# Four heads to a score unit, local mixes by two pairs, and feed-forward parts as streams of their own

## What is computed

```
# ATTN0, ATTN1: 16 heads of 8 channels
scores = einsum('bhqd,bhkd->bhqk', q, k) * scale      # ATTN1: rotary q and k, causal
out = softmax(scores) @ v
# LOCAL0, LOCAL1: 8 heads of 64 channels
h = shift_token(x); q, k, v = split(h @ wqkv)
q = l2norm(q) * qs; k = l2norm(k) * ks; q, k = rotary_xpos(q, k)
x = x + local_attention(q, k, v) @ wo
h = layernorm(shift_token(x)) * lg + lb
a, g = split(h @ w1 + b1); x = x + (a * gelu(g)) @ w2 + b2
```

## Time and profile before

| | |
|---|---|
| median of three runs | 3128.42 us (3126.73 to 3133.96) |
| profiled execution, its own time | 3130.85 us |
| its span, first to last instruction | 3128.7 us |
| granted clock of TensorE, mean | 0.957 |
| busy: TensorE, VectorE, ScalarE, GpSimd | 2816.9, 2411.2, 2147.9, 1548.2 us |

### The profile page before, as it was taken

How to read it: one execution, slowest core, us unless ns; L and a number is a source line. 1 busy time by engine, 2 the same in 40 slices (tenths; PEclk the granted TensorE clock), 3 DMA queues, 4 the chain that set the end, 5 groups by cost and what they waited for, 6 DMA issues and landing times.

```text
span 3128.7 us, 65895 instructions
## 1 busy us (share of the span) xinstructions
PE 2816.9 (90%) x22656; PEld 1976.8 (63%) x22656; DVE 2411.2 (77%) x6016; ACT 2147.9 (69%) x5956; POOL 1548.2 (49%) x1741
## 2 busy tenths in 40 slices
PE   3678999999999999999999999999999999998875
PEld 1455666666666666666666666666666666666553
DVE  3367888888888888888888888878888888777653
ACT  2356777777777777677777767777776777776653
POOL 1034554555545455554555554545555555545542
PEclk7689999999999999999999999999999999999987
DMA  2000000000000000000000000000000000000000
GB/s 67 3 3 4 5 6 6 5 6 6 6 5 7 6 4 6 6 6 6 5 7 6 5 6 6 6 5 7 6 5 6 6 6 5 6 4 4 4 5 5
DMA packets 41974, 21.76 MB, mean 7 GB/s; under 512 B 21131, under 2 KB 41013, under 8 KB 41653
## 3 DMA queue, kind: packets, MB, share of 16 engines
q1 hardware_dynamic: 41652, 17.55, 2.0%
HBM read 9.17 MB, written 4.19 MB: 4 GB/s over the span
## 4 chain that ended last, share of the span: by engine, by line
PE 43%; DVE 27%; ACT 19%; POOL 5%; issue 4%; DMA 0%; DVEq 0%; POOLq 0%; SPq 0%
DVE negmax L836 10%; ACT rawP L730 6%; ACT P L730 5%; PE bank L1050 5%; PE bank L1143 5%; PE bank L1151 4%; PE bank L1030 4%; PE bank L1096 3%; DVE ss L879 3%; PE bank L1159 3%; POOL rn L633 3%; PE bank L1130 2%; ACT probs L697 2%; PE bank L1085 2%; PE bank L1011 2%
## 5 line engine op out<-in xcount | busy, mean ns | idle before, releaser
L836 DVE TENSOR_REDUCE negmax<-bank 128x2 f32<-128x512 f32 (+1 forms) x896 | 554.4, 679 | 25.7 <-PE bank L1011 25.6
L697 ACT ACTIVATE probs<-bank 128x512 f32<-128x512 f32 (+1 forms) x1024 | 480.9, 568 | 131.8 <-PE bank L1030 129.5
L633 POOL TENSOR_TENSOR rn<-ss,minus_half 128x16 f32<-128x16 f32 x128 | 372.6, 2911 | 172.0 <-DVE ss L894 171.4
L582 POOL TENSOR_TENSOR veps<-moments,eps_tile 128x2 f32<-128x2 f32 x192 | 38.2, 199 | 785.4 <-DVE moments L788 785.4
L1085 PE MATMUL bank<-wqkv_sb,hS 128*128 128x512 f32 x768 | 390.9, 625 | 30.9 <-ACT P L730 12.7
L914 DVE TENSOR_REDUCE negmax<-bank 128x2 f32<-128x384 f32 (+1 forms) x384 | 211.7, 593 | 135.1 <-PE bank L1118 133.4
L600 POOL TENSOR_SCALAR_AFFINE_SELECT probs<-probs 128x256 f32<-128x256 f32 x512 | 225.2, 463 | 166.8 <-ACT probs L697 166.4
L1050 PE MATMUL bank<-probs,V 128*16 128x256 f32 (+1 forms) x4096 | 259.5, 373 | 24.4 <-ACT probs L697 22.2
L1011 PE MATMUL bank<-kT,qT 32*128 32x256 f32 (+1 forms) x2048 | 216.8, 324 | 25.7 <-DVE negmax L836 16.1
L1085 PEld LDWEIGHTS bank<-wqkv_sb,hS 128*128 128x128 f32 x768 | 131.9, 193 | 163.3 <-issue 125.6
L730 ACT ACTIVATE rawP<-bank,negmax 128x128 f32<-128x128 f32 x512 | 179.7, 376 | 79.7 <-DVE negmax L914 79.7
(11 more groups left out here) (138 smaller groups left out, 7299.2 us busy)
## 6 DMA issues: line engine op xcount, KB each, us to landing
xin<-x SPq DMA_DIRECT2D x32, 128.0 KB, 2.1
out<-xout SPq DMA_DIRECT2D x32, 128.0 KB, 1.8
V<-YB SPq DMA_DIRECT2D x64, 63.5 KB
wqkv_sb<-wqkv SPq DMA_DIRECT2D x1, 1536.0 KB
V<-YB SPq DMA_DIRECT2D x64, 0.2 KB
w_sb<-w SPq DMA_DIRECT2D x1, 682.0 KB
w_sb<-w SPq DMA_DIRECT2D x2, 256.0 KB
wo_sb<-wo SPq DMA_DIRECT2D x2, 256.0 KB
```

What stands on the lines that cost most here:

```text
L633: nc.gpsimd.tensor_tensor(rn[:, l, t].rearrange("p m h -> p (m h)"), ss[:, l, t].rearrange("p m h -> p (m h)"), minus_half[:], ALU.pow).th ...
L697: nc.scalar.activation(dst, src, ACT.Exp, scale=SCALE0 if k == ATTN0 else SCALE1)\
L836: nc.vector.reduce_max(negmax[:, k, t, head:head + 4 * many - 3:4], tile(u, e)[:, :].rearrange("p (h k) -> p h k", h=many), AX.X, negate=T ...
```

## The change

STREAMS becomes 6: the feed-forward parts of the local layers are streams FEED0 and FEED1, with buffers of their own (feed_h, feed_hT, up2T), and the gates are written into up2T. `maxes` and `scores` take four heads and four banks in a unit, so ATTN0 has four `maxes` instead of eight, ATTN1 three instead of six, and both have four `scores` instead of eight. `scores2` is a unit of two banks and one of four instead of three of two. `mix2` takes two pairs of heads, 512 columns of a bank, in two units instead of four. The clamp of the sums of squares is a maximum over pairs, of which the second element is a constant 1e-24, written to another tile. One more sequence is kept in XB and YB. All orders and bank lists are new; FIRST, TURNS and LAST have 472, 159 and 482 units in place of 339, 180 and 561, and ROUNDS is 26. The strings are cut here except for the start of TensorE's TURNS, and so are loops that change only in their bounds.

```diff
-STREAMS = 4
+STREAMS = 6
...
-KEPT_X, KEPT_Y = 5, 3
+KEPT_X, KEPT_Y = 6, 4
...
-ATTN0, ATTN1, LOCAL0, LOCAL1 = range(STREAMS)
...
-ROUNDS = 27
+ATTN0, ATTN1, LOCAL0, LOCAL1, FEED0, FEED1 = range(STREAMS)
...
+ROUNDS = 26
...
 TURNS = {
     "tensor": (
-        "1110330102222111002022103333333332222221122222200022011102333333333000313113100013333332222000332203"
-        "20033311111331220000322200122222201111222222333313000330011101333100033301222223"
+        "3333022222211222221120001130231011101333333003323002222220444433111110044341142222222233130000333330"
+        "01110112000001555553330500550222222333330211122020251333333"
...
-    units += [Unit("maxes", u, bank=2) for u in range(6 if rotary else 8)]
+    units += [Unit("maxes", u, bank=4) for u in range(3 if rotary else 4)]
     units += [Unit("negmax", m_hi=1, m_ready=1)]
     units += [Unit("turn_q", u, source="with maxima", bank=1) for u in range(2)]
+
+    def scores(g):
+        return Unit("scores", g, bank=4, **(dict(masked=4) if rotary else {}))
+
+    def mix(g):
+        return Unit("mix", g, bank=1)
+
     for g in range(GROUPS):
-        units += [Unit("scores", 2 * g + n, bank=2, **(dict(masked=2) if rotary else {})) for n in range(2)]
-        units += [Unit("mix", g, bank=1)]
+        units += [scores(g), mix(g)]
...
-def local_units(last):
+def local_units():
...
-    units += [Unit("scores2", u, bank=2, max_done=2) for u in range(3)]
+    units += [Unit("scores2", 0, bank=2, max_done=2), Unit("scores2", 1, bank=4, max_done=4)]
...
-    units += [turn_p(0), turn_p(1), turn_p(2), turn_p(3), mix2(0), turn_p(4), turn_p(5), mix2(1),
-              turn_p(6), turn_p(7), mix2(2), mix2(3)]
+    units += [turn_p(u) for u in range(4)] + [mix2(0)] + [turn_p(u) for u in range(4, 8)] + [mix2(1)]
     units += [Unit("project2", bank=1)]
-    units += [Unit("shift_rows", rows_in=2 * 16, rows_left=1)]
-    units += norm_units("h")
+    return units
+
+
+def feed_units(last):
+    units = [Unit("shift_rows", rows_in=2 * 16, rows_left=1)] + norm_units("h")
...
-    if k == ATTN1 and part < 2:
-        return 0, 0, GROUPS, part
-    n = part + 2 if k == ATTN1 else part
-    return n // 4, 2 * (n // 2 % 2), 2, n % 2
+    if k == ATTN1 and part == 0:
+        return 0, 0, GROUPS
+    n = part + 1 if k == ATTN1 else part
+    return n // 2, 2 * (n % 2), 2
...
-        ss = sb("ss", [P, 2, TT, 2, HEADS])
+        ss = sb("ss", [P, 2, TT, 2, HEADS, 2])
+        ss_kept = sb("ss_kept", [P, 2, TT, 2, HEADS])
...
-        up2T = rawA[:, :, 0:3 * SEQ].rearrange("p l (c q) -> p l c q", c=3)
+        feed_h = sb("feed_h", [P, 2, TT, DIM])
+        feed_hT = sb("feed_hT", [P, 2, SEQ])
+        up2T = sb("up2T", [P, 2, len(HTILES), SEQ])
...
-                    for sem, count in newest(taken(earlier(u, "project2"))):
+                    for sem, count in newest(taken(fellow(u, LOCAL0 + l, "project2")), taken_by_last(u, "down2")):
...
-                    flat = ss[:, l, t].rearrange("p m h -> p (m h)")
                     dve.wait_ge(sig("sums", src), so_far("sums", src) + 1)
-                    nc.vector.tensor_scalar(flat, flat, 1e-24, None, ALU.max).then_inc(sig("ss_ready", u), 1)
+                    nc.vector.reduce_max(ss_kept[:, l, t].rearrange("p m h -> p (m h)"), ss[:, l, t].rearrange("p m h e -> p (m h) e"), AX.X)\
+                        .then_inc(sig("ss_ready", u), 1)
...
+                elif u.kind == "mix2":
+                    dve.wait_ge(has_filled(u), uses(u))
+                    nc.vector.tensor_copy(o2T[:, l, 2 * u.part:2 * u.part + 2, :].rearrange("p c q -> p (c q)"), tile(u)[:])\
+                        .then_inc(has_emptied(u), 1)
...
-                    t, first, many, pair = max_part(k, u.part)
-                    for e in range(2):
-                        head = 4 * first + 2 * pair + e
+                    t, first, many = max_part(k, u.part)
...
                     for i in range(many):
-                        for e in range(2):
-                            rows = slice(32 * (2 * pair + e), 32 * (2 * pair + e) + 32)
+                        for e in range(4):
+                            rows = slice(32 * e, 32 * e + 32)
                             last = mm(tile(u, e)[:, i * keys:(i + 1) * keys], qT[rows, k, first + i, t * P:(t + 1) * P],
...
-                    g, pair = u.part // 2, u.part % 2
+                    g = u.part
...
-                        for sem, count in newest(*of("scores", 2 * g, 2 * g + 1)):
+                        for sem, count in newest(*of("scores", g)):
                             pe.wait_ge(sem, count)
                     else:
-                        pe.wait_ge(sig("masked", u), so_far("masked", u))
+                        src = earlier(u, "scores", g)
+                        pe.wait_ge(sig("masked", src), so_far("masked", src) + 4)
...
-                    for sem, count in newest(*(of("qkv2", 2, 5) if n == 0 else []), *of("turn_p", 2 * n, 2 * n + 1), free(u)):
-                        pe.wait_ge(sem, count)
-
-
-                    for q0, w, t, c0 in ((0, P + WINDOW, 0, 0), (P, P, 1, P + WINDOW)):
-                        for e in range(2):
-                            hd = 2 * n + e
-                            last = mm(tile(u)[64 * e:64 * e + 64, q0:q0 + w], V2[:, l, t, hd * HD:(hd + 1) * HD],
-                                      probs2[l][n % 2][:, e, c0:c0 + w], start=t == 0, stop=t == 1, skip_group_check=True)
+                    for sem, count in newest(*(of("qkv2", 2, 5) if n == 0 else []), *of("turn_p", *range(4 * n, 4 * n + 4)), free(u)):
+                        pe.wait_ge(sem, count)
+
+
+                    for i in range(2):
+                        for q0, w, t, c0 in ((0, P + WINDOW, 0, 0), (P, P, 1, P + WINDOW)):
+                            for e in range(2):
+                                hd = 4 * n + 2 * i + e
+                                at = i * SEQ + q0
+                                last = mm(tile(u)[64 * e:64 * e + 64, at:at + w], V2[:, l, t, hd * HD:(hd + 1) * HD],
+                                          probs2[l][i][:, e, c0:c0 + w], start=i == 0 and t == 0, stop=t == 1, skip_group_check=True)
```

275 lines of the change are left out of this document (141 added, 134 removed).

## The result

The changed kernel takes 3142.75 us (median of 8 runs, 3130.75 to 3145.66) against 3127.57 for the kernel before on the same chips: a ratio of 1.0043, 95% interval 1.0028 to 1.0059. It is slower by a little more than the 0.2% that can be told from nothing; 2970 us was predicted. The profiled execution took 3142.88 us.

A forecast was written before the change was run, and what follows sets the result against it. TensorE was taken to bound two thirds of a round, VectorE the rest. Work 79.2 + idle 7.0 + clock 1.2 = 87.4 us a round; fill 385 + rounds 2272 + drain 315 = 2972, said as 2970 us, range 2885 to 3060.

The forecast's parts named there:

- What bounds the kernel: Clean round of 89.6 us: TensorE bounds two thirds, VectorE the 29-us stretch with the maxima; local streams' latency a third limit.
- Part 1: Four heads at once on TensorE: 5.7 us less work a round, 84.9 to 79.2, by overlapping strips and fewer shape changes.
- Part 2: Smaller edits off TensorE's path: mix copies, clamp; VectorE 75.0 to about 73.5 us a round; 35 us if VectorE bound throughout.
- Part 3: Feed-forward as own streams: opens LOCAL's closed loop of 89.6 us a round and shortens the drain, 48 us taken.
- Part 4: Four-bank units' waits for free banks: 0.9, 2.0 and 0.8 us idle on TensorE, together 3.7 a round; elsewhere 0 to 3.
- term of idle time: TensorE's idle time in a clean round: 7.0 us instead of 4.7.
- The clock's 1.2 us: Mean round over clean round, put down to stretches at 1.2 GHz instead of 2.4; taken to stay at 1.2 us.
- The fill: Time before the steady rounds: 2.97 rounds of 87.4 us plus 125, 385 us; longer than 400 would show the forecast wrong.
- B: Rival: larger bank waits and VectorE's maxima stretch bind, about 2 us a round arrive, 3017 to 3036 us; chance 0.16.
- D: Rival: slower through four-bank waits, ten more short-reuse units a round, 3202 us at 0.8 us each; chance 0.10.
- E: Rival: strips overlap no better than now, or gain and waits cancel; no change, 3128 us; chance 0.02.

The follow-up runs named there:

- b_half: The kernel before, with half of the products of its 16-head maxes and scores units left out on TensorE: 3120.11 us, ratio 0.9991.
- b_look: The kernel before, with VectorE's maxima reductions looking at half of the keys: 3022.21 us, ratio 0.9670.
- a_pairs: The changed kernel, its four-bank units issuing heads 0 and 1 first, then 2 and 3: 3143.61 us, ratio 1.0051 to the kernel before.
- a_qkv: The changed kernel, with the local layers' first product in bfloat16 instead of float32: 3163.00 us, ratio 1.0138 to the kernel before.
- a_each: The changed kernel, its four-bank units waiting for each bank just before that bank's first product: 3141.71 us, ratio 1.0056 to the kernel before.
- b_qkv: The kernel before, with the local layers' first product in bfloat16 instead of float32: 3183.43 us, ratio 1.0204.
- b_qkv4: b_qkv with each of those bfloat16 products issued four times over, as useless work: 3123.40 us, ratio 1.0004 to the kernel before.
- a_keep: The changed kernel, with useless products laid into TensorE's waits of 0.9 and 2.0 us: 3164.25 us, ratio 1.0135 to the kernel before.

## Why the prediction was wrong

**What bounds the kernel: this step failed.** It read one 29-us stretch as VectorE's and the other two thirds of the round as TensorE's, because TensorE was busy there 58.8 of 60.6 us. Busy isn't bound: VectorE was 97% busy over 45 us. In b_half 1.9 us less TensorE work shortened the full-clock round by 0.3, and in the changed kernel, whose orders differ too, 5.5 us less shortened it by nothing, while 6.8 us less VectorE work (b_look) shortened it by 2.2. The chain's 43% for TensorE misled in the same way: b_half took 63 us off lines of that chain for nothing.

**Part 1** was right in size: 84.9 to 79.4 us a round (79.2 predicted), eight products in 0.44 us (timeline after):

```profile
1595.92 0.51 PE L1033 MATMUL bank<-kT,qT 32*128 32x256 f32 x8
1596.36 0.66 PE L1119 MATMUL bank<-ident_r,rawA 128*128 128x128 f32 x4
```

Its reason was half right: the order of heads plays no part (a_pairs).

**Part 2** had the direction, and the saving is nearly twice as large: VectorE 75.0 to 72.2 (73.5 predicted). The clamp (52.1 to 22.3 us in the kernel) and the mix copies (99.4 to 87.1) save what was forecast; another 31 us went from a multiplication that the change leaves as it is (rawA by rn, L902 before, 1185 to 947 ns each). It was costed as "not on TensorE's path", and in the kernel before the clamp turned out worth 21 us of the whole; in the new orders it is worth nothing. The step's figure for a VectorE-bound kernel, 35 us, was nearer than its verdict.

**Part 3** held in the drain and failed in the round. The last LOCAL1 took 46.6 us to its projection (about 45 predicted). In the rounds the loop closed again: LOCAL1's shift, its projection and its next shift, after:

```profile
1752.09 0.38 ACT L686 ACTIVATE hS<-bank 64x256 f32<-64x256 f32 x1
...
1843.22 0.38 ACT L686 ACTIVATE hS<-bank 64x256 f32<-64x256 f32 x1
...
1843.61 0.41 DVE L896 TENSOR_TENSOR YB<-bank,YB 128x256 f32<-128x256 f32 x1
```

91.5 us from shift to projection, where it was 64.8 with 28.8 of feed-forward behind it. The stream filled the round without its feed-forward part. Whether that is cause or consequence no run tells; a lighter product at its head (a_qkv) didn't help, in a run in which all of the middle 24 rounds had a stretch at half clock.

**Part 4** had the right place and the right first two waits (0.9 and 2.0; 0.88 and 1.99 measured). The third, put at 0.8 us for ScalarE, was 0.37 ahead of L1052, and not for ScalarE. **Its term of idle time failed**: 10.4 us, not 7.0. It walked one chain of bank waits and let "0 to 3" stand for the rest. The rest was 7.4: nine waits of 0.4 to 1.1 us and three smaller, two thirds of it in VectorE's stretch and 5.2 us for VectorE. The prediction's own mark, "wrong if the round is not under 88", was met.

**The clock's 1.2 us**, carried over unchanged, is 91.45 - 89.8 = 1.65 after. **The fill** came out at 423 us, beyond the mark of 400: 2.97 x 91.45 + 125 = 397 by its own formula, so of the 38 us about 12 come of the longer round and about 27 of the fill itself.

**Rivals.** B named the mechanism, VectorE's stretch, and still let 2 us arrive; 0 did. The rule of the Trainium skill (TensorEngine Tiling (Array Packing), section PSUM Bottleneck) that stood beside B, that copying out of PSUM may become the limit, agrees with the runs: only the kernels with a shorter reduction out of PSUM show the change's gain. D had the sign, by waits for four banks; by a_each the wait for all four at once is worth only 0.2 to 0.5 us a round of it. E, "the gain and the waits cancel", had 0.02 and came nearest: 5.5 us gained, 5.7 lost.

What stays open is why a full-clock round is 90 us at all: 6.8 us off VectorE shorten it by 2.2, 5.5 off TensorE by nothing, so neither of these two alone holds it, and which hand-overs do wasn't measured. No run took work off GpSimd, which had 5% of the chain before and is 82 us busier in the changed kernel (1548.2 to 1630.2), where no change was forecast. Nor did a run change the feed-forward streams alone.

## What to carry to other kernels

Before costing work taken off the busiest engine, take a like amount off each engine in turn, one short run each: here 219 us off VectorE brought 103 (some of it by the clock), 179 off ScalarE 22, and 63 off TensorE nothing, at busy shares of 77, 69 and 90%. Compare the rounds at equal granted clock too, since a gain can be hidden by the clock, as in a_each. In a kernel whose engines run in orders written out beforehand, bigger units mean fewer and longer hand-overs; when the consumer needs 2.5 us for what the producer makes in 0.5, a faster producer waits. Where TensorE's clock is at stake, look at the granted clock round by round and at the waits ahead of each fall, since a lighter TensorE can be the slower one.

## What the runs showed of the hardware that I hadn't expected

- 250 us less TensorE work in one product cost 2% (b_qkv), and the same time came back with useless products (b_qkv4). In the changed kernel the clock fell behind waits of 0.88 and 1.99 us, with no long idle time. The Trainium skill (TensorE: Matmul & The Clock Gate, section A second HAM failure mode: psum-queue depth-cycling) tells of a kernel whose short idle times between groups of products made the clock go up and down; this trace agrees, and with these two waits mostly filled (a_keep) the time at half clock went from 327 to 202 us.
- A tensor_scalar of 128 columns took 350 or 1129 ns, by what GpSimd did beside it. The Trainium skill (SBUF — State Buffer, section Who interferes with whom) says that a tensor_scalar in a two-port mode and a GpSimd instruction exclude each other for a whole instruction; the trace agrees in that all 112 slow ones overlapped a GpSimd instruction, and over the kernel this line took 219 us of VectorE against 156 in the changed kernel. No trace shows the mode.
- Eight products on four row strips took 0.44 us whether the heads were taken in turn or by pairs.
